# Activation transposes of 40 chunks moved from TensorE to VectorE blocks and a trip through DRAM, with each down product one step later

## The chip, the cores and the metric

The kernel runs on one core of a Trainium2 chip. The metric is device time in microseconds (us) of one execution, the median of several. A profile is one further execution, taken with the hardware profiler. TensorE's matmuls appear as PE, its weight loads as PEld, VectorE as DVE, ScalarE as ACT, GpSimd as POOL and the queue of DMA issues of SyncE as SP.

## The reference

`x` is 64 batches of 32 rows with 512 columns, so 2048 rows of 512 in float32. Four residual stages follow each other; each adds its result to x. What matters here is the first:

```
gate = x @ W_gate.T + 0.5 * (x @ A_gate[b].T) @ B_gate[b].T     # F = 1376 columns
up   = x @ W_up.T   + 0.5 * (x @ A_up[b].T)   @ B_up[b].T
act  = silu(gate) * up
x    = x + act @ W_down.T + 0.5 * (act @ A_down[b].T) @ B_down[b].T
```

`b` picks one of 16 adapters of rank 16 for each batch. Then come a 32x32 mix of the rows of a batch by one of 16 matrices, a 512x512 product with two of eight gated experts of rank 16, and a second 32x32 mix.

## The kernel before

The 2048 rows are 16 tiles (`NT`) of 128 rows, four batches each. The 1376 columns of the hidden layer are three chunks (`CHUNKS`, `NC` = 3): n = 0 has 352 columns (three pieces of 128, 128 and 96), n = 1 and n = 2 have 512 (four pieces of 128). A step `s` is one chunk of one tile, 48 steps in all; the first six (`FREE`) run in an order of their own, then s = 3i + n.

Every product is made of three matmuls on high and low parts of both operands (`product`), because each operand is split into a rounded high part, which ScalarE casts (`hi`), and the remainder, which VectorE subtracts (`lo`). The stationary operand is loaded anew for each of the three.

A step on TensorE is `gate` (12 matmuls), `up` (12), `adapters` (4, after which the chunk's gate and up values are complete, `s_gu`), and then for a finished chunk the product with W_down. ScalarE applies silu to the gate half, VectorE multiplies by the up half. The result `act` has rows on partitions and hidden columns in the free dimension, but the down product contracts over hidden columns. So `transpose_act` turns each piece with a TensorE transpose against the identity into PSUM (`act_t`), ScalarE and VectorE split it into `act_hl` (two buffers), and `down` uses the pieces as stationary operands: two halves of `down_ps`, three matmuls each, 288 columns wide. In step s TensorE transposes chunk s-1 in the middle and multiplies it by W_down at the end. After a tile's third chunk, `mask_td`, `transpose_td` and `down_adapters` add the rank-16 part and VectorE adds the residual (`x1`).

The order is written out by hand. `lane_jobs(s)` is the list of jobs that ScalarE and VectorE both follow, in that order; `gathers(s)` is GpSimd's list of indirect loads (`b` the adapter's B columns, `a` its A matrices, `bd` its B_down, `w13` the mixing matrices), followed on GpSimd by the low part of one tile's mixing matrix (`low_bd`, steps 10 to 25). SyncE's queue issues the plain transfers in program order and stops at each wait: `store_bd` (steps 10 to 25) waits for `low_bd`, `store_tile` for a tile's residual. From step 45 on the loads for the second part of the kernel are issued there.

Of the kernel before, what the change touches and what calls it, by code (L numbers as in the profile page):

```python
# [123 lines left out]

PLAIN = NT - 3
# [17 lines left out]
def down_no(s):  # L143

    i, n = ORDER[s]
    return i * NC + n

# [41 lines left out]
def gathers(s):  # L189

    if s < FREE:
        return {-1: a_items(0, 0) + [("b", 0), ("b", 1)] + a_items(1) + a_items(0, 1),
                0: [("b", 2)],
                1: [("b", 3)],
                2: [("bd", 0), ("b", 4)],
                3: [("b", 5)] + a_items(2),
                4: [("b", 6)],
                5: [("bd", 1)]}[s]
    i, n = ORDER[s]
    out = []  # L200
    if s + 1 < STEPS:
        out.append(("b", s + 1))
    if n < 2 and i + 1 < NT:
        out += a_items(i + 1)[n * TB // 2:(n + 1) * TB // 2]
    if n == 2:
        out.append(("bd", i))
    if 0 <= s - W13_FIRST < NT:
        out.append(("w13", s - W13_FIRST))
    return out


def lane_jobs(s):
# [17 lines left out]
    i, n = divmod(s, NC)  # L230
    jobs = []
    if n == 0:
        if i < NT:
            jobs.append(("tm", i))
        jobs.append(("act", s - 1))
        if i < NT:
            jobs += [("t", i), ("bd", i - 1), ("tdm", i - 1), ("gate", s), ("b", s + 1)]
        else:
            jobs += [("bd", i - 1), ("tdm", i - 1), ("td", i - 1), ("x1", i - 1)]
    elif n == 1:  # L240
        jobs += [("td", i - 1), ("act", s - 1), ("x1", i - 1)]
        if i + 1 < NT:
            jobs.append(("x", i + 1, 0))
        jobs += [("gate", s), ("b", s + 1)]
    else:
        jobs.append(("act", s - 1))
        if i + 1 < NT:
            jobs.append(("at", i + 1))
        jobs.append(("gate", s))
        if i + 1 < NT:  # L250
            jobs += [("b", s + 1), ("adt", i + 1)]
    return jobs
# [5 lines left out]
def bass_conditioned_residual_chain(nc, x_t, x_rows, it_cond, it_lang, wgu, wd, a_all, a_gu, a_d, b_d,  # L258
# [6 lines left out]
    with ExitStack() as ctx:  # L265
# [25 lines left out]
        x_scratch = nc.dram_tensor("x_after_l0", [ROWS, H], F32, kind="Internal").ap()  # L291
        bd_scratch = nc.dram_tensor("bd13", [NT, P, 4 * P], F32, kind="Internal").ap()
# [29 lines left out]
        act_hl = sb("act_hl", [2, 2, HC, P], F32R, mem_a)  # L322
# [99 lines left out]
        s_actt = sem("s_actt")  # L422
        s_hi = sem("s_hi")
# [80 lines left out]
        def act_of(s):  # L504
            w = width(ORDER[s][1])
            return act[:, slot(s), 0:w] if slot(s) < 2 else x_res[:, 1, 0:w]

# [79 lines left out]
        def _(sp):  # L587
# [45 lines left out]

            for s in range(-1, STEPS):
# [29 lines left out]
                if s == 5:  # L664
                    store_tile(0)
                    sp.wait_ge(s_actt, down_no(2) + 1)
                    sp.dma_start(x_res[:, 1, :], x_rows[P:2 * P, :]).then_inc(s_xin[1], 16)
                if s >= FREE:
                    i, n = ORDER[s]
                    if n == 1:  # L670
                        store_tile(i - 1)
                    if n == 2:
# [111 lines left out]
        def _(sc):  # L784
# [15 lines left out]
            def job_hi(job):  # L800
# [3 lines left out]
                if kind == "gate":  # L804
                    s = job[1]
                    sc.wait_ge(s_gu, s + 1)
                    if slot_before(s) is not None:
                        sc.wait_ge(s_actt, down_no(slot_before(s)) + 1)
                    sc.activation(act_of(s), gate_of(s), ACT.Silu).then_inc(s_silu, 1)  # L809
                elif kind == "act":  # L810
                    d = job[1]
                    sc.wait_ge(s_actt, d + 1)
# [119 lines left out]
        def _(ve):  # L932
# [64 lines left out]

            def job_lo(job):
# [14 lines left out]
                if kind == "gate":  # L1013
# [3 lines left out]
                    ve.tensor_tensor(a, a, up_of(s), ALU.mult).then_inc(s_mul, 1)  # L1017
                    return
                ve.wait_ge(s_hi, split_no[job])
                if kind == "act":  # L1020
                    d = job[1]
                    for k, j0, j1 in act_blocks(d):
# [158 lines left out]
        def _(pe):  # L1181
# [66 lines left out]
            def transpose_act(d):  # L1248
# [3 lines left out]
                if d >= 1:  # L1252
                    pe.wait_ge(s_lo, s_lo_of(("act", d - 1)))
# [5 lines left out]
            def down(d):  # L1259
# [9 lines left out]
                for j, f in enumerate(pieces_of(n)):  # L1269
# [3 lines left out]
                    a_hl = [act_hl[0:w, d % 2, part, j, :] for part in range(2)]  # L1273
# [139 lines left out]
            for s in range(FREE + 1, STEPS):  # L1413
                i, n = ORDER[s]
                gate(s, 0, HC // 2)
                if n == 1:
# [4 lines left out]
                if n == 1:  # L1421
# [112 lines left out]
```

## Time and profile before

| what | value |
|---|---|
| median of 3 runs | 579.16 us (578.42 to 579.67) |
| the profiled execution's own time | 578.63 us |
| its span, first to last instruction | 576.5 us |
| mean granted TensorE clock | 1.000 |
| PE busy | 566.9 us (98%) |
| DVE, ACT, POOL busy | 303.0, 205.1, 224.7 us |

The own time is 2.1 us longer than the span, and the median lies 0.5 us above the own time. The engines' busy times overlap. A busy PE is not PE at its best rate: matmuls are pipelined, so how often one starts tells more than how long one lasts.

### The profile page before, as it was taken

What the parts mean: (1) busy time and instruction counts of PE and PEld (TensorE: products, weight loads), DVE (VectorE), ACT (ScalarE), POOL (GpSimd) and SP (SyncE); (2) the same over time, 40 slices, a digit from 0 to 9 for tenths busy, and PEclk for the clock granted to TensorE, in tenths of its full rate; (3) what the DMA queues carried; (4) which work ended last, traced back from release to release, by engine and by line L of the source; (5) the groups of instructions that cost most, each with busy time, mean ns of one, the idle gap of its engine ahead of it and who ended that gap; (6) DMA issues with size and microseconds to landing.
All of it is one profiled execution on the core that took longest, in us unless ns stands there. A gap on an engine that the chain in (4) does not pass through costs nothing.

```text
span 576.5 us, 8783 instructions
## 1 busy us (share of the span) xinstructions
PE 566.9 (98%) x3367; PEld 513.1 (89%) x3367; DVE 303.0 (53%) x695; ACT 205.1 (36%) x413; POOL 224.7 (39%) x229
## 2 busy tenths in 40 slices
PE   6999999999999999999999999999999999999997
PEld 6889989898989898989898989898989899999995
DVE  6797344444444444444444444444444667777876
ACT  5774233333333333332323232323232533333330
POOL 5751053747474747341414141414140212443430
PEclk9999999999999999999999999999999999999999
DMA  8983352444444444452424242424241821234322
GB/s 296 362 265 121 109 163 78 143 135 141 135 143 134 143 135 142 132 157 76 139 78 138 77 139 76 139 77 138 77 139 73 305 81 55 74 133 143 110 92 74
DMA packets 34585, 77.38 MB, mean 134 GB/s; under 512 B 5232, under 2 KB 8944, under 8 KB 34544
## 3 DMA queue, kind: packets, MB, share of 16 engines
q0 software_dynamic: 10880, 37.23, 20.7%
q1 hardware_dynamic: 23520, 39.54, 20.2%
q8 instruction: 27, 0.44, 0.3%
q14 instruction: 14, 0.11, 0.1%
q10 hardware_dynamic: 144, 0.04, 0.0%
HBM read 64.22 MB, written 12.58 MB: 133 GB/s over the span
## 4 chain that ended last, share of the span: by engine, by line
PE 92%; DVE 3%; POOL 2%; DMA 2%; issue 1%; ACT 0%; DVEq 0%; ACTq 0%
PE gu_ps L1186 13%; PE gu_ps L1185 13%; PE gu_ps L1184 13%; PE down_ps L1184 8%; PE down_ps L1185 8%; PE down_ps L1186 8%; PE l_ps L1184 5%; PE l_ps L1185 5%; PE l_ps L1186 5%; PE act_t L1256 3%; PE gu_ps L1192 3%; PE gu_ps L1191 3%; POOL a_raw L696 1%; PE x2t_ps L1310 1%; DMA a_raw<-a_all,idx_batch 1%; DVE w_sb L971 1%
## 5 line engine op out<-in xcount | busy, mean ns | idle before, releaser
L696 POOL DMA_INDIRECT b_sel_raw<-b_gu,idx_rank x48 | 47.3, 985 | 184.5 <-PE gu_ps L1192 174.0
L1184 PE MATMUL down_ps<-wd_sb,act_hl 128*128 128x288 f32 (+1 forms) x352 | 105.0, 298 | 0.2 <-DVE wd_sb L971 0.2
L1184 PE MATMUL gu_ps<-w_sb,xt 128*128 128x512 f32 x256 | 104.2, 407 | 0.0
L1185 PE MATMUL down_ps<-wd_sb,act_hl 128*128 128x288 f32 (+1 forms) x352 | 103.8, 295 | 0.0
L1186 PE MATMUL down_ps<-wd_sb,act_hl 128*128 128x288 f32 (+1 forms) x352 | 103.6, 294 | 0.0
L1186 PE MATMUL gu_ps<-w_sb,xt 128*128 128x512 f32 x256 | 100.8, 394 | 0.0
L1185 PE MATMUL gu_ps<-w_sb,xt 128*128 128x512 f32 x256 | 100.5, 393 | 0.0
L696 POOL DMA_INDIRECT a_raw<-a_all,idx_batch x60 | 71.8, 1197 | 52.1 <-DVE wd_sb L971 38.1
L818 ACT CAST act_hl<-act_t 128x256 fp32r<-128x256 f32 (+1 forms) x64 | 27.3, 453 | 132.2 <-PE act_t L1256 130.9
L809 ACT ACTIVATE act<-gu_ps 128x512 f32<-128x512 f32 (+1 forms) x47 | 26.1, 555 | 124.0 <-PE gu_ps L1192 124.0
L971 DVE TENSOR_TENSOR act_hl<-act_t,act_hl 128x256 fp32r<-128x256 f32 (+1 forms) x64 | 32.0, 521 | 71.2 <-ACT act_hl L818 71.1
L1184 PEld LDWEIGHTS down_ps<-wd_sb,act_hl 128*128 128x128 f32 (+1 forms) x352 | 66.1, 188 | 1.9 <-DVE wd_sb L971 0.6
L1185 PEld LDWEIGHTS down_ps<-wd_sb,act_hl 128*128 128x128 f32 (+1 forms) x352 | 66.1, 188 | 1.2
L1186 PEld LDWEIGHTS down_ps<-wd_sb,act_hl 128*128 128x128 f32 (+1 forms) x352 | 66.0, 188 | 0.0
L1017 DVE TENSOR_TENSOR act<-act,gu_ps 128x512 f32<-128x512 f32 (+1 forms) x47 | 29.8, 634 | 66.5 <-ACT act L809 66.5
L971 DVE TENSOR_TENSOR b_sel<-b_sel_raw,b_sel 128x1024 fp32r<-128x1024 f32 (+1 forms) x48 | 53.6, 1116 | 10.5 <-ACT b_sel L793 10.5
L1186 PEld LDWEIGHTS gu_ps<-w_sb,xt 128*128 128x128 f32 x256 | 48.0, 187 | 10.7
L1184 PEld LDWEIGHTS gu_ps<-w_sb,xt 128*128 128x128 f32 x256 | 48.1, 188 | 8.4
L1185 PEld LDWEIGHTS gu_ps<-w_sb,xt 128*128 128x128 f32 x256 | 48.3, 189 | 7.2
L793 ACT CAST b_sel<-b_sel_raw 128x1024 fp32r<-128x1024 f32 (+1 forms) x48 | 45.7, 952 | 1.5 <-DMA b_sel_raw<-b_gu,idx_rank 1.3
L1184 PE MATMUL l_ps<-w2ra_hl,x2t_hl 128*128 128x328 f32 (+1 forms) x128 | 41.6, 325 | 0.4 <-issue 0.2
L1185 PE MATMUL l_ps<-w2ra_hl,x2t_hl 128*128 128x328 f32 (+1 forms) x128 | 39.7, 310 | 0.0
(150 smaller groups left out, 1093.6 us busy)
## 6 DMA issues: line engine op xcount, KB each, us to landing
xt_raw<-x_t SPq DMA_DIRECT2D x16, 256.0 KB, 2.5
w_sb_raw<-wgu SPq DMA_DIRECT2D x16, 256.0 KB, 7.5
x_res<-x_rows SPq DMA_DIRECT2D x16, 256.0 KB, 2.9
x_after_l<-x_res SPq DMA_DIRECT2D x16, 256.0 KB, 2.3
bd<-bd_hl SPq DMA_DIRECT2D x16, 256.0 KB, 2.0
x<-x_after_l SPq DMA_DIRECT2D x16, 256.0 KB, 2.8
bd_hl<-bd SPq DMA_DIRECT2D x16, 256.0 KB, 3.9
out<-y SPq DMA_DIRECT2D x15, 256.0 KB, 2.0
```

The costliest lines, as they stand in the source:

```text
L696: nc.gpsimd.indirect_dma_start(out=dst, out_offset=None, in_=table, in_offset=bass.IndirectOffsetOnAxis(ap=idx, axis=0)).then_inc(s, 16)
L793: sc.copy(out_, in_).then_inc(s_hi, 1)
L809: sc.activation(act_of(s), gate_of(s), ACT.Silu).then_inc(s_silu, 1)
L818: ins = sc.copy(act_hl[0:k, d % 2, 0, j0:j1, :], act_t[0:k, j0:j1, :])
L971: return ve.tensor_tensor(out_, raw, high.bitcast(F32), ALU.subtract)
L1017: ve.tensor_tensor(a, a, up_of(s), ALU.mult).then_inc(s_mul, 1)
L1184: pe.matmul(out_, stationary[0], moving[0], start=start, stop=False, skip_group_check=True)
L1185: pe.matmul(out_, stationary[0], moving[1], start=False, stop=False, skip_group_check=True)
L1186: return pe.matmul(out_, stationary[1], moving[0], start=False, stop=stop, skip_group_check=True)
L1191: pe.matmul(out_, stationary, moving[0], start=False, stop=False, skip_group_check=True)
L1192: return pe.matmul(out_, stationary, moving[1], start=False, stop=True, skip_group_check=True)
L1256: mm = pe.transpose(act_t[0:w, j, :], act_of(s)[:, j * P:j * P + w], ident)
```

## The change

`MOVED` is range(6, 46): chunks 6 to 45, 40 of the 48. For them TensorE's transpose is gone. Behind the multiplication VectorE transposes `act` in square blocks of 32x32 (`blocks`) into `act_blk`, which is the other slot of `act`; all moved chunks now use slot 1. A block transpose leaves each value in its group of 32 partitions. SyncE's queue therefore writes the result to DRAM (`act_scratch`, 128 rows of 512 numbers, 256 KB) and, when this has landed, reads it back in four transfers, one for each group of 32 partitions (`move_act`), each row in runs of 128 numbers (512 bytes). It arrives in the low half of `act_hl`, ScalarE casts the high part from there, and VectorE subtracts in place. In a row of the result the pieces alternate: number 4n + j belongs to row n of piece j, so `stationary_of` reads a stationary operand with a step of four numbers (16 bytes), where `act_hl` before had its 128 numbers side by side. Chunks with three pieces leave every fourth place unused.

In step s TensorE now multiplies chunk s-2 by W_down instead of s-1. The tile's end (`td`, `down_adapters`, `x1`, `store_tile`) moves from n = 1 to n = 2 of the next tile, the split of `bd` from n = 0 to n = 1, and its gather on GpSimd from the step n = 2 of its own tile to n = 0 of the next, behind that step's `a` gathers.

```diff
+MOVED = range(FREE, STEPS - 2)
@@ gathers
-    if n == 2:
+    if n == 0 and i >= 3:
+        out.append(("bd", i - 1))
+    if s == STEPS - 1:
         out.append(("bd", i))
@@ lane_jobs
+    last = [("act", s - 1)] if s - 1 not in MOVED else []
+    acts = ([("act", s - 2)] if s - 2 in MOVED else []) + last
+        return [("tm", i)] + acts + [("t", i), ("gate", s), ("b", s + 1)]
+        return acts + x + ([("bd", i - 1)] if i > 2 else []) + [("gate", s)] + tdm + [("b", s + 1)]
+    jobs = [("td", i - 1)] + acts[:1] + [("x1", i - 1)] + acts[1:]
@@ stationary and split
+        def stationary_of(d, part, j, w):
+            a = act_hl[0:w, d % 2, part, :, :]
+            if d in MOVED:
+                return a.rearrange("p a n -> p (a n)").rearrange("p (n j) -> p j n", j=HC)[:, j, :]
+            return a[:, j, :]
@@ sync
+            def move_act(d):
+                sp.wait_ge(s_blocks, moved(d))
+                if d - 2 in MOVED:
+                    sp.wait_ge(*act_in(d - 2))
+                sp.dma_start(act_scratch[d % 2, :, :], act_blk).then_inc(s_aout, 16)
+                if d >= 2:
+                    sp.wait_ge(s_d, d - 1)
+                sp.wait_ge(s_aout, 16 * moved(d))
+                for j in range(HC):
+                    rows = slice(j * CH, (j + 1) * CH)
+                    sp.dma_start(act_raw[rows, d % 2, 1, :, :],
+                                 act_scratch[d % 2, :, j * P:(j + 1) * P].rearrange("(b f) n -> f b n", b=TB)
+                                 ).then_inc(s_ain[d % 2], 16)
+                if s - 1 in MOVED:
+                    move_act(s - 1)
@@ scalar
+                    if d in MOVED:
+                        sc.wait_ge(*act_in(d))
+                        cols = split_cols(d)
+                        hi(cols(act_hl[:, d % 2, 0, :, :]), cols(act_raw[:, d % 2, 1, :, :]))
+                        return
@@ vector
+            def blocks(s):
+                ve.wait_ge(s_mul, s + 1)
...
+                    ve.wait_ge(s_aout, 16 * moved(s - 1))
...
+                by_place = act_blk.rearrange("p (j r a) -> p j a r", j=TB, a=HC)
+                ins = ve.transpose(by_place[:, :, 0:full, :],
+                                   act_of(s)[:, 0:whole_cols].rearrange("p (a j f) -> p j a f", j=TB, f=CH))
...
+                    if s in MOVED:
+                        blocks(s)
@@ tensor, the loop over steps
-                if n == 1:
+                if n == 2:
                     transpose_td(i - 1)
-                transpose_act(s - 1)
+                if s == STEPS - 1:
+                    transpose_act(s - 1)
-                down(s - 1)
+                if s - 2 in MOVED:
+                    down(s - 2)
                 if n == 0:
                     adapters(s)
+            down(STEPS - 2)
```

On TensorE, in the middle of a step with n = 0, between the last gate matmuls (`gu_ps_0`) and the first up matmuls (`gu_ps_1`), before:

```order
L1184 MATMUL gu_ps_0<-wg_sb,xt 128x480
L1185 MATMUL gu_ps_0<-wg_sb,xt 128x480
L1186 MATMUL gu_ps_0<-wg_sb,xt 128x480
L1256 MATMUL act_t<-ident_sb,act 128x128 x4
L1184 MATMUL gu_ps_1<-wu_sb,xt 128x352
L1185 MATMUL gu_ps_1<-wu_sb,xt 128x352
```

The same engine near the end of such a step in the changed kernel, from the last up matmuls through the transpose of the adapters' part to the down product:

```order
L1269 MATMUL gu_ps_1<-wu_sb,xt 128x352
L1270 MATMUL gu_ps_1<-wu_sb,xt 128x352
L1271 MATMUL gu_ps_1<-wu_sb,xt 128x352
L1319 MATMUL t_ps<-ident_sb,t_m 128x128 x2
L1269 MATMUL down_ps<-wd_sb,act_hl 128x288
L1270 MATMUL down_ps<-wd_sb,act_hl 128x288
L1271 MATMUL down_ps<-wd_sb,act_hl 128x288
```

The transposes into `act_t` have gone from these steps; the down product stands where it stood, and is that of the chunk one earlier.

On SyncE's queue, one tile in the part where mixing matrices are stored (`bd<-bd_hl`), before:

```order
L615 DMA xt_raw<-x_t 128x512
L625 DMA bd<-bd_hl 128x512 x2
L590 DMA x_after_l<-x_res 128x512
L625 DMA bd<-bd_hl 128x512
L674 DMA x_res<-x_rows 128x512
```

and in the changed kernel, where `act_blocks` is the DRAM buffer:

```order
L650 DMA xt_raw<-x_t 128x512
L660 DMA bd<-bd_hl 128x512
L674 DMA act_blocks<-act 128x512
L680 DMA act_hl_raw<-act_blocks 32x4x128 x4
L660 DMA bd<-bd_hl 128x512
L674 DMA act_blocks<-act 128x512
L680 DMA act_hl_raw<-act_blocks 32x4x128 x4
L660 DMA bd<-bd_hl 128x512
L674 DMA act_blocks<-act 128x512
L680 DMA act_hl_raw<-act_blocks 32x4x128 x4
L625 DMA x_after_l<-x_res 128x512
L725 DMA x_res<-x_rows 128x512
```

Five issues have been added for each chunk, each group of them behind the store of a mixing matrix.

On GpSimd, the step n = 0 of the changed kernel in that part (its first row waits for the adapters' matmuls of the step ahead, its second for VectorE's split of the A matrices):

```order
L747 DMA b_sel_raw<-b_gu,idx_rank 128x1024
L747 DMA a_raw<-a_all,idx_batch 128x304 x2
L747 DMA bd_hl_raw<-b_d,idx_rank 128x512
L747 DMA w_raw<-w,idx_ch 128x64
L802 TENSOR_TENSOR bd_hl<-bd_raw,bd_hl 128x256
```

Before, the gather `bd_hl_raw` stood in the step n = 2, which has no `a_raw` gathers. The last row is `low_bd`, for which the store on SyncE waits.

## Rows read from the trace of the kernel before

**Rows 1.** The page: its head and first section, busy time by engine.

```profile
span 576.5 us, 8783 instructions
PE 566.9 (98%) x3367; PEld 513.1 (89%) x3367; DVE 303.0 (53%) x695; ACT 205.1 (36%) x413; POOL 224.7 (39%) x229
```

**Rows 2.** The longest wait of TensorE's matmuls: total us, times, longest.

```profile
PE gu_ps L1184 <- DVE wg_sb L971: 5.5, 1, 5.5
```

**Rows 3.** Busy time by engine in one tile's window (PE, PEld, DVE, ACT, POOL).

```profile
130.92:159.66 28.74, 28.74 (x169) 25.81 (x168) 12.48 (x22) 9.80 (x20) 16.97 (x20) 1.00 0.44 139
```

**Rows 4.** One of TensorE's groups by shape: busy us, mean ns, idle before.

```profile
L1256 PE MATMUL act_t<-ident_sb,act 128*128 128x128 f32 x158 | 24.9, 272 | 0.0
```

**Rows 5.** Timeline of TensorE around one group of transposes: start, us, instruction.

```profile
210.25 0.38 PE L1185 MATMUL gu_ps<-wg_sb,xt 128*128 128x480 f32 x1
210.47 0.38 PE L1186 MATMUL gu_ps<-wg_sb,xt 128*128 128x480 f32 x1
210.68 0.60 PE L1256 MATMUL act_t<-ident_sb,act 128*128 128x128 f32 x4
211.04 0.41 PE L1184 MATMUL gu_ps<-wu_sb,xt 128*128 128x352 f32 x1
211.28 0.32 PE L1185 MATMUL gu_ps<-wu_sb,xt 128*128 128x352 f32 x1
211.44 0.32 PE L1186 MATMUL gu_ps<-wu_sb,xt 128*128 128x352 f32 x1
```

**Rows 6.** Timeline of TensorE, three regular stretches: 128, 288 and 512 columns wide.

```profile
24.97 0.27 PE L1185 MATMUL down_ps<-wg_sb,xt 128*128 128x128 f32 x1
...
26.09 0.27 PE L1186 MATMUL down_ps<-wg_sb,xt 128*128 128x128 f32 x1
...
213.39 0.30 PE L1185 MATMUL down_ps<-wd_sb,act_hl 128*128 128x288 f32 x1
...
215.89 0.29 PE L1186 MATMUL down_ps<-wd_sb,act_hl 128*128 128x288 f32 x1
...
220.75 0.40 PE L1186 MATMUL gu_ps<-w_sb,xt 128*128 128x512 f32 x1
220.98 0.39 PE L1184 MATMUL gu_ps<-w_sb,xt 128*128 128x512 f32 x1
```

**Rows 7.** Timeline of ScalarE: the silu at the start of a step n = 0.

```profile
118.69 0.60 ACT L809 ACTIVATE act<-gu_ps 128x512 f32<-128x512 f32 x1 [2.57 <-PE gu_ps L1192]
```

**Rows 8.** Timeline of VectorE behind that silu.

```profile
119.32 0.69 DVE L1017 TENSOR_TENSOR act<-act,gu_ps 128x512 f32<-128x512 f32 x1 [2.40 <-ACT act L809]
125.58 0.69 DVE L971 TENSOR_TENSOR act_hl<-act_t,act_hl 128x512 fp32r<-128x512 f32 x1 [0.57 <-ACT act_hl L818]
130.28 0.36 DVE L991 TENSOR_TENSOR td<-down_ps,head_sb 128x64 f32<-128x64 f32 x2 [1.58 <-PE down_ps L1186]
```

**Rows 9.** Timeline of GpSimd in the same step, and one bd gather later.

```profile
118.93 0.98 POOL L696 DMA_INDIRECT b_sel_raw<-b_gu,idx_rank  x1 [2.99 <-PE gu_ps L1192]
122.02 0.95 POOL L696 DMA_INDIRECT a_raw<-a_all,idx_batch  x1 [2.12 <-DVE wd_sb L971]
...
125.48 0.76 POOL L751 TENSOR_TENSOR bd_hl<-bd_raw,bd_hl 128x256 fp32r<-128x256 f32 x1
...
140.53 1.36 POOL L696 DMA_INDIRECT bd_hl_raw<-b_d,idx_rank  x1 [0.30 <-issue]
```

**Rows 10.** Timeline of SyncE's queue: two merged stores, and one load.

```profile
126.26 12.28 SPq L625 DMA_DIRECT2D bd<-bd_hl  x2
...
144.28 0.43 SPq L674 DMA_DIRECT2D x_res<-x_rows  x1
```

**Rows 11.** DMA issues by line: count, size, median us from issue to landing.

```profile
x_res<-x_rows SPq DMA_DIRECT2D x16, 256.0 KB, 2.9
x_after_l<-x_res SPq DMA_DIRECT2D x16, 256.0 KB, 2.3
bd_hl<-bd SPq DMA_DIRECT2D x16, 256.0 KB, 3.9
```

More of the change, by code:

```diff
@@ L146, in down_no, with pe_transposed @@
     return i * NC + n
+def pe_transposed(d):
+    return sum(k not in MOVED for k in range(d + 1))
 def gu_done(i):
@@ L230, in lane_jobs @@
     i, n = divmod(s, NC)
-    jobs = []
+    last = [("act", s - 1)] if s - 1 not in MOVED else []
+    if i == NT:
+        return last + [("bd", i - 1), ("tdm", i - 1), ("td", i - 1), ("x1", i - 1)]
+    acts = ([("act", s - 2)] if s - 2 in MOVED else []) + last
     if n == 0:
[L233 to L252, printed above, removed]
+        return [("tm", i)] + acts + [("t", i), ("gate", s), ("b", s + 1)]
+    if n == 1:
+        x = [("x", i + 1, 0)] if i + 1 < NT else []
+        tdm = [("tdm", i - 1)] if i > 2 else []
+        return acts + x + ([("bd", i - 1)] if i > 2 else []) + [("gate", s)] + tdm + [("b", s + 1)]
+    jobs = [("td", i - 1)] + acts[:1] + [("x1", i - 1)] + acts[1:]
+    if i + 1 < NT:
+        return jobs + [("at", i + 1), ("gate", s), ("b", s + 1), ("adt", i + 1)]
+    return jobs + [("gate", s)]
 NO_SPLIT = ("gate", "tm", "tdm", "x1")
@@ L321, in bass_conditioned_residual_chain @@
             pass
-        act_hl = sb("act_hl", [2, 2, HC, P], F32R, mem_a)
+        act_hl, act_raw = sb_raw("act_hl", [2, 2, HC, P], mem_a)
         b_sel, b_raw = sb_raw("b_sel", [2, 2, 2 * H], mem_a)
@@ L422, in bass_conditioned_residual_chain @@
         s_actt = sem("s_actt")
+        s_blocks = sem("s_blocks")
+        s_aout = sem("s_aout")
+        s_ain = [sem(f"s_ain{i}") for i in range(2)]
         s_hi = sem("s_hi")
@@ L505, in act_of, with moved, act_in, split_cols @@
             w = width(ORDER[s][1])
+            if s in MOVED:
+                return act[:, 1, 0:w]
             return act[:, slot(s), 0:w] if slot(s) < 2 else x_res[:, 1, 0:w]
+        act_blk = act[:, 0, :]
+        def moved(d):
+            return d - MOVED[0] + 1
+        def act_in(d):
+            return s_ain[d % 2], 16 * TB * sum(k % 2 == d % 2 for k in MOVED if k <= d)
+        def stationary_of(d, part, j, w):
[3 more added lines that the diff above has]
+            return a[:, j, :]
+        def split_cols(d):
+            n = len(pieces_of(d % NC))
+            def cols(a):
+                return a.rearrange("p a n -> p (a n)").rearrange("p (n j) -> p n j", j=HC)[:, :, 0:n]
+            return cols
         def base_cols(i):
@@ L806, in job_hi @@
                     sc.wait_ge(s_gu, s + 1)
-                    if slot_before(s) is not None:
+                    if s - 1 in MOVED and s in MOVED or s == STEPS - 2:
+                        sc.wait_ge(s_blocks, moved(s - 1))
+                    elif s == STEPS - 1:
+                        sc.wait_ge(s_aout, 16 * len(MOVED))
+                    elif slot_before(s) is not None:
                         sc.wait_ge(s_actt, down_no(slot_before(s)) + 1)
@@ L811, in job_hi @@
                     d = job[1]
-                    sc.wait_ge(s_actt, d + 1)
+                    if d in MOVED:
[3 more added lines that the diff above has]
+                        return
+                    sc.wait_ge(s_actt, pe_transposed(d))
                     if d == 0:
@@ L996, in mask_td @@
                 ins.then_inc(s_tdm, 1)
+            def blocks(s):
+                ve.wait_ge(s_mul, s + 1)
+                if s == MOVED[0]:
+                    ve.wait_ge(s_actt, s)
+                else:
+                    ve.wait_ge(s_aout, 16 * moved(s - 1))
+                whole_cols = width(ORDER[s][1]) // P * P
+                by_place = act_blk.rearrange("p (j r a) -> p j a r", j=TB, a=HC)
+                full = whole_cols // P
+                ins = ve.transpose(by_place[:, :, 0:full, :],
+                                   act_of(s)[:, 0:whole_cols].rearrange("p (a j f) -> p j a f", j=TB, f=CH))
+                left = width(ORDER[s][1]) - whole_cols
+                if left:
+                    ins = ve.transpose(by_place[:, 0:left // CH, full, :],
+                                       act_of(s)[:, whole_cols:].rearrange("p (j f) -> p j f", f=CH))
+                ins.then_inc(s_blocks, 1)
             def job_lo(job):
@@ L1017, in job_lo @@
                     ve.tensor_tensor(a, a, up_of(s), ALU.mult).then_inc(s_mul, 1)
+                    if s in MOVED:
+                        blocks(s)
                     return
@@ L1021, in job_lo @@
                     d = job[1]
+                    if d in MOVED:
+                        cols = split_cols(d)
+                        lo(cols(act_hl[:, d % 2, 1, :, :]), cols(act_raw[:, d % 2, 1, :, :]),
+                           cols(act_hl[:, d % 2, 0, :, :])).then_inc(s_lo, 1)
+                        return
                     for k, j0, j1 in act_blocks(d):
@@ L1251, in transpose_act @@
                 pe.wait_ge(s_mul, s + 1)
-                if d >= 1:
-                    pe.wait_ge(s_lo, s_lo_of(("act", d - 1)))
+                before = max((k for k in range(d) if k not in MOVED), default=None)
+                if before is not None:
+                    pe.wait_ge(s_lo, s_lo_of(("act", before)))
                 for j, f in enumerate(pieces_of(n)):
@@ L1272, in down @@
                         pe.wait_ge(s_lo, s_lo_of(("wd", f)))
-                    a_hl = [act_hl[0:w, d % 2, part, j, :] for part in range(2)]
+                    a_hl = [stationary_of(d, part, j, w) for part in range(2)]
                     for half in range(2):
```

6 lines of the change are left out of this document (3 added, 3 removed).

## The prediction

> **What bounds the kernel now.** I read the page's first section, then TensorE's waits, then its groups and timeline. TensorE is busy for 566.9 of 576.5 us [rows 1], and its waits come to five entries, of which one, at the start, has 5.5 us and the others 0.2 us each [rows 2]. In one tile's window of 28.74 us it is busy for all of it, while VectorE has 12.48 us of work, ScalarE 9.80 and GpSimd 16.97 [rows 3]. So an instruction taken off TensorE in the middle of the kernel shortens the kernel by the time for which it held up the next matmul, as long as nothing that TensorE needs then comes later. What the other engines get is free while they keep their slack.
>
> That time isn't the 272 ns of one transpose [rows 4], since starts overlap. In the timeline the last of the 480-wide matmuls starts at 210.47 and the second 352-wide one at 211.28, so 0.81 us later, with four transposes between [rows 5]. The same step costs 0.22 us behind a 480-wide matmul (210.25 to 210.47) and 0.16 behind a 352-wide one (211.28 to 211.44), so 0.38 without them. The four cost 0.43 us, 0.108 each. The other group of spacings that I need: a 128-wide matmul with its own weight load starts every 0.112 us (ten steps from 24.97 to 26.09), a 288-wide one of the down product every 0.132 (19 steps from 213.39 to 215.89), and a 512-wide one every 0.23 [rows 6].
>
> **Removed.** Chunks 6 to 45 are 14 with three pieces and 26 with four: 42 + 104 = 146 transposes. At 0.108 us this is 15.8 us. All of it is on the path.
>
> **Unchanged in number.** The down products keep their matmuls. The casts and subtractions have about the size that they had; a three-piece chunk has one of each in place of two.
>
> **Added on VectorE.** One block transpose of 512 numbers per partition for each chunk (two instructions where there are three pieces). No row has one. The nearest are the 128x512 multiplication and subtraction, 0.69 us each [rows 8]; I take 0.7. From below, nothing; from above, twice 0.69, since it writes with a step of four numbers. Three per tile are 2.1 to 4.2 us on top of 12.48 in a window of 28.74, so VectorE stays far from full. The job behind it in the step n = 1 is `td`, 0.36 us [rows 8], which TensorE's `transpose_td` needs 1.4 us (six 512-wide matmuls) after the down product ends. Multiplication and transpose lie beside that product (24 matmuls, 3.2 us): 0.6 for silu, 0.7, 0.7, and VectorE is free 1.2 us before `td` may start. With a transpose of over 1.9 us this cover begins to go, and with over 2.9 TensorE waits.
> The Trainium skill (VectorE: DVE Perf Modes, The three transpose paths) gives 311 ns for a 128x128 block transpose of 2-byte numbers and says that it stays within 32x32 blocks; no run here shows it, and the sum doesn't use it.
>
> **Added transfers.** 256 KB out and 256 KB in per chunk, about 9.6 us apart, so 53 GB/s beside the 139 of the window [rows 3]. A 256 KB store takes 2.3 us to landing, loads 2.9 to 3.9 [rows 11]. Does the chunk arrive before its down product? With d the chunk's adapters' end as zero, the product one step later starts for a chunk n = 2 after 18 down matmuls (2.4), gate and up of n = 0 (12 x 0.22 + 12 x 0.16 = 4.5), two transposes (0.2), 24 down matmuls (3.2), four adapter matmuls (0.6), and gate, up and adapters of n = 1 (28 x 0.23 = 6.4): 17.3 us. In the later part of the kernel the chain is silu, multiplication, transpose (2.0), store (2.3 and 0.4 to issue), four issues of 0.43 [rows 10], landing (2.9), cast (0.6) and subtraction (0.7): 10.6 us. That leaves more than 6 us, so no wait.
>
> In steps 10 to 25 SyncE's queue has the store of a mixing matrix ahead of the chunk, and that waits for GpSimd's `low_bd`. It is issued at 126.26, 7.6 us behind the silu at 118.69 [rows 7, 10]. In the changed kernel the `a` gather, which waits for VectorE and sat 2.12 us [rows 9], comes 0.7 later because of the block transpose, and the `bd` gather now stands in this step, 1.36 and 0.30 us [rows 9]. So the store is issued at 9.9, the chunk's at 10.3, lands at 12.6; four issues bring 14.3; landing 17.2; cast 17.8; subtraction 18.5 less the 0.3 by which neighbours on two engines overlap, 18.2. Needed at 17.3, and 17.4 with rounding: TensorE waits about 0.8 us. This happens for n = 2 alone, in five tiles: a chunk n = 0 has neither that wait nor the bd gather ahead of its store, a chunk n = 1 no a gathers. So I charge 4 us. From below: with 2.3 us for the load 0.3 us a tile, 1.5 in all. From above: 3.9 us for each transfer and 1.4 for the block transpose give 4.1 us a tile, 20 in all; that would need each of them at its worst, and I take 10 as this case's end.
>
> **What the down matmul's weight load costs.** Each of the 146 pieces is loaded six times, 876 loads, now with a step of 16 bytes. No row has such a load. What the rows show is the room: loads side by side keep up with a start every 0.112 us, and a down matmul starts every 0.132 [rows 6]. So a load may grow by 20 ns for nothing. At 876 x 18 ns = 15.8 us the whole gain is eaten, which is a load of 0.150 us. From below, nothing. From above, a doubled load: 0.224 against 0.132, 876 x 0.092 = 81 us. In favour of nothing: the moving operand of the same engine is read at 512 numbers in 0.23 us, 2.2 a nanosecond [rows 6], the weights at no more than 128 in 0.112, 1.1 a nanosecond, so the load uses half of the rate that the reads next to it show. Against: that fast read takes four numbers of each 16 bytes, one new 16 bytes every 1.8 ns, and the strided load would need a new one every 0.9 ns. Between ends so far apart I take nothing, being nearer to the row for the same operation, and hold the doubling as the chief rival.
> The Trainium skill speaks against the change here (Advanced Engine Details and Errata, Memory Cachelines): SBUF lines are 16 bytes, and at least two hits on a line are needed to absorb the access latency. By that rule every number of these loads would be a line of its own, with a penalty whose size the page doesn't give. No run so far shows it for weights.
>
> **Sum.** 15.8 off, 4.0 on, nothing for the loads: -11.8 us. The profiled execution goes from 578.63 to 566.8 and its span from 576.5 to 564.7. The median of the runs is 0.5 above the profiled execution, so 567.3 us. The end of the kernel keeps its order but for one product; the queued loads for the second part go ahead of chunk 45, which has 18 us until its product, and I charge nothing.
>
> **The rivals.** (A) The forecast: weight loads hide, few waits. Own range 563.4 (no waits at all) to 573.4; chance 0.55.
> (B) Slower: the strided weight load takes twice as long and becomes the pace of the down product, at the places of the 876 matmuls. It decides from 0.150 us a load on. -15.8 + 81 + 0 (the waits vanish because the product is later) = +65: 644 us. For it speaks that nothing in the trace covers more than 20 ns; against it the spare rate. Chance 0.27. Between (A) and (B), a load of 0.140 to 0.20 us gives -9 to +44; chance 0.08, of which a quarter ends faster and a quarter within 0.2%.
> (C) The way through DRAM is late in every step, not only in 15: SyncE's queue stops for each landing, and each transfer takes 3.9 us or more. For it speaks the full queue in steps 10 to 25; against it the 6 us of slack after. If the two earlier kinds of chunk in those steps wait as well, 1.5 us each, that adds 15 us: 579 to 582. Chance 0.07, half of it within 0.2% or slower.
> (D) The transposes did not matter: they hide in TensorE's own pipeline. The 0.43 us in the timeline say no; 0.03.
>
> **How the numbers follow.** A change of 0.2% (1.2 us) is about what can be told from none. Faster: 0.55 + 0.02 + 0.03 = 0.60, rounded up by what lies between to 0.61; same: 0.02 + 0.02 = 0.04; slower: the rest, 0.35. The likeliest case gives 567.3. Its own range is 563.4 to 573.4, which holds 0.55 alone, so the range must reach to (B), up to 645; it leaves out little but a load that more than doubles.
>
> **What would show it.** TensorE busy for about 551 us. Starts of down matmuls 0.132 us apart as before under (A), 0.2 or more under (B); the recorded time of a weight load tells nothing by itself, since it contains latency. Waits of TensorE on the low half of `act_hl`, about 0.8 us in tiles 4 to 8 and none later; a block transpose of 0.7 to 1.4 us; the chunk's store issued 2.5 us behind its silu in late steps and 10 us in the five early ones. The prediction is wrong if the spacing of the down product changes, or if TensorE waits in the later tiles.

## The result and the profile after

The changed kernel takes 653.45 us (median of four runs, 652.87 to 654.84), the kernel before 578.92 beside it (four runs). The ratio is 1.129 with an interval of 1.1266 to 1.1313: 74.5 us slower, where 567.3 was forecast and 645 was the upper end of the range. The page's head and first section, against [rows 1]:

```profile
span 651.0 us, 8755 instructions
PE 638.0 (98%) x3221; PEld 586.1 (90%) x3221; DVE 333.4 (51%) x735; ACT 202.7 (31%) x399; POOL 209.1 (32%) x229
```

The 146 matmuls are gone (3367 to 3221), and TensorE is busy for 71.1 us more, at a mean granted clock of 0.997. So nearly all of the time went into work that takes longer, not into waits. The waits of TensorE's matmuls (total us, times, longest), against [rows 2]:

```profile
PE gu_ps L1269 <- DVE wg_sb L1031: 5.4, 1, 5.4
PE l_ps L1269 <- POOL x_hl L807: 2.6, 1, 2.6
```

One wait of size is new: 2.6 us at the start of the second part, on GpSimd's low half of `x_hl`. The other entries have 0.5 us or less each, and none is on `act_hl`. The timeline of TensorE, one down product, against [rows 6]:

```profile
278.27 0.30 PE L1269 MATMUL down_ps<-wd_sb,act_hl 128*128 128x288 f32 x1
278.40 0.40 PE L1270 MATMUL down_ps<-wd_sb,act_hl 128*128 128x288 f32 x1
...
283.54 0.40 PE L1271 MATMUL down_ps<-wd_sb,act_hl 128*128 128x288 f32 x1
283.77 0.40 PE L1269 MATMUL gu_ps<-w_sb,xt 128*128 128x512 f32 x1
```

From 278.40 to 283.54 there are 22 steps, so a start every 0.2336 us where there was one every 0.132. A 288-wide matmul now keeps the pace of a 512-wide one (0.23). Only the first step, from 278.27 to 278.40, still has 0.13. The operation that changed shows in the view of the tile `act_hl` (duration min/median/max in ns, first and last start, forms): its weight loads.

```profile
L1269 PEld LDWEIGHTS down_ps<-wd_sb,act_hl x352: 186/329/334, 37.2 to 548.5; 128*128 128x128 f32 x160, 96*128 96x128 f32 x16
```

The shortest, 186 ns, belongs to the chunks whose operand still lies side by side; the median of 329 is the strided form. The sum closes: 876 loads x 0.1015 us is 88.9, less 15.8 for the transposes, plus the new wait of 2.6, gives 75.7, and 74.5 was measured. If in each of the 40 products one step keeps its 0.13 us, 836 loads pay: 84.9, and 71.7 in all, to which the clock (0.997 over 651.0 us) adds 2.0 at most.

### The profile page after: what moved, and what is told of

Same layout as the page of the kernel before. It is cut to its first block, busy times and chain, and to the rows that moved or that the text cites. A ratio compares the mean times of both kernels' runs of the same rounds, so it can differ in the third digit from the quotient of the medians.

```text
span 651.0 us, 8755 instructions
## 1 busy us (share of the span) xinstructions
PE 638.0 (98%) x3221; PEld 586.1 (90%) x3221; DVE 333.4 (51%) x735; ACT 202.7 (31%) x399; POOL 209.1 (32%) x229
## 4 chain that ended last, share of the span: by engine, by line
PE 90%; DMA 3%; POOL 2%; DVE 2%; SPq 1%; issue 1%; ACT 0%; DVEq 0%; ACTq 0%
PE down_ps L1270 11%; PE down_ps L1271 11%; PE down_ps L1269 11%; PE gu_ps L1269 11%; PE gu_ps L1271 11%; PE gu_ps L1270 11%; PE l_ps L1269 4%; PE l_ps L1270 4%; PE l_ps L1271 4%; PE gu_ps L1277 3%; PE gu_ps L1276 3%; DMA act_blocks<-act 1%; POOL a_raw L747 1%; PE x2t_ps L1396 1%; DMA b_sel_raw<-b_gu,idx_rank 1%
## 5 line engine op out<-in xcount | busy, mean ns | idle before, releaser
L1270 PE MATMUL down_ps<-wd_sb,act_hl 128*128 128x288 f32 (+1 forms) x352 | 133.5, 379 | 0.0
L1271 PE MATMUL down_ps<-wd_sb,act_hl 128*128 128x288 f32 (+1 forms) x352 | 133.4, 379 | 0.0
L1269 PE MATMUL down_ps<-wd_sb,act_hl 128*128 128x288 f32 (+1 forms) x352 | 132.8, 377 | 0.3 <-DVE wd_sb L1031 0.3
L1269 PEld LDWEIGHTS down_ps<-wd_sb,act_hl 128*128 128x128 f32 (+1 forms) x352 | 106.7, 303 | 2.3 <-DVE wd_sb L1031 0.7
L1271 PEld LDWEIGHTS down_ps<-wd_sb,act_hl 128*128 128x128 f32 (+1 forms) x352 | 107.6, 306 | 0.0
L1270 PEld LDWEIGHTS down_ps<-wd_sb,act_hl 128*128 128x128 f32 (+1 forms) x352 | 107.1, 304 | 0.2
L747 POOL DMA_INDIRECT a_raw<-a_all,idx_batch x60 | 61.2, 1021 | 64.6 <-DVE wd_sb L1031 50.6
L1269 PE MATMUL l_ps<-w2ra_hl,x2t_hl 128*128 128x328 f32 (+1 forms) x128 | 41.6, 325 | 0.4 <-issue 0.2
L1068 DVE STREAM_TRANSPOSE act<-act 128x512 f32<-128x512 f32 (+1 forms) x40 | 38.1, 952 | 7.0 <-DMA act_blocks<-act 5.8
L1270 PE MATMUL l_ps<-w2ra_hl,x2t_hl 128*128 128x328 f32 (+1 forms) x128 | 39.7, 310 | 0.0
L1271 PE MATMUL l_ps<-w2ra_hl,x2t_hl 128*128 128x328 f32 (+1 forms) x128 | 39.6, 310 | 0.0
```

Of the source, the lines that this page charges most:

```text
L747: nc.gpsimd.indirect_dma_start(out=dst, out_offset=None, in_=table, in_offset=bass.IndirectOffsetOnAxis(ap=idx, axis=0)).then_inc(s, 16)
L1068: ins = ve.transpose(by_place[:, :, 0:full, :], act_of(s)[:, 0:whole_cols].rearrange("p (a j f) -> p j a f", j=TB, f=CH))
L1269: pe.matmul(out_, stationary[0], moving[0], start=start, stop=False, skip_group_check=True)
L1270: pe.matmul(out_, stationary[0], moving[1], start=False, stop=False, skip_group_check=True)
L1271: return pe.matmul(out_, stationary[1], moving[0], start=False, stop=stop, skip_group_check=True)
```

## The experiments

Each group of runs has its own runs of the kernel before: 579.41 for the first four kernels, 578.81 for the next four, 578.99 for the last two. Two theories stood against each other. L: every one of the 876 loads costs 0.1 us because of its step of 16 bytes, and the rest of the change costs little. T: the rest of the change (256 KB out to DRAM and back in each step, over the same buffers and queues) slows the down product or makes it wait.

**The changed kernel with operands side by side.** `stationary_of` and the split of `act_hl` no longer use the step:

```diff
             a = act_hl[0:w, d % 2, part, :, :]
-            if d in MOVED:
-                return a.rearrange("p a n -> p (a n)").rearrange("p (n j) -> p j n", j=HC)[:, j, :]
             return a[:, j, :]
...
-            n = len(pieces_of(d % NC))
+            n = HC
```

> The changed kernel in which the down product of the moved chunks reads each stationary operand as 128 numbers side by side (step of 4 bytes instead of 16), and the split always covers all four places; the operands are then in the wrong order, so the output is not the reference's. Theory 1 (the 16-byte step of the weight load makes it the pace of the down product): its matmuls start every 0.132 us again instead of 0.233, and the time is that of before less 15.8 us for the transposes plus a few us of waits, 563 to 570 us. Theory 2 (something else in the changed kernel slows the down product: operands that arrive by DMA, reads of act_hl by three engines at once, the later place in the order): the spacing stays at 0.233 and the time near 653 us.

Measured: 583.89 us (580.92 to 586.66), ratio 1.0078 (1.004 to 1.0116). Down matmuls start 0.13 us apart again (two rows of TensorE's timeline), so L holds for the 71 us of busy time:

```profile
172.62 0.29 PE L1267 MATMUL down_ps<-wd_sb,act_hl 128*128 128x288 f32 x1
172.75 0.29 PE L1268 MATMUL down_ps<-wd_sb,act_hl 128*128 128x288 f32 x1
```

But 583.89 is above the 563 to 570 of the expectation, and 20 us above what the removal alone should leave. The waits of TensorE and of SyncE's queue in this kernel (the profiled execution is the longest of the four, 586.66 us):

```profile
PE down_ps L1267 <- DVE act_hl L1029: 10.5, 6, 2.6
...
PE gu_ps L1274 <- DVE b_sel L1029: 2.5, 1, 2.5
...
SPq L675 <- DMA act_blocks<-act: 120.6, 40, 6.1
```

The 10.5 us on `act_hl` are the wait that the forecast had priced at 4.0. Five of the six are on a chunk n = 2, as forecast, with 2.56, 1.27, 2.35, 2.33 and 1.84 us. The timeline of ScalarE, SyncE's queue and TensorE in one of these steps:

```profile
115.95 0.60 ACT L862 ACTIVATE act<-gu_ps 128x512 f32<-128x512 f32 x1 [2.77 <-PE gu_ps L1275]
126.17 0.33 SPq L658 DMA_DIRECT2D bd<-bd_hl  x1
126.59 0.38 SPq L672 DMA_DIRECT2D act_blocks<-act  x1
128.98 1.74 SPq L678 DMA_DIRECT2D act_hl_raw<-act_blocks  x4
...
132.91 0.39 PE L1275 MATMUL gu_ps<-b_sel,t_hl 128*128 128x512 f32 x1
...
134.46 0.62 ACT L842 CAST act_hl<-act_hl_raw 128x512 fp32r<-128x512 f32 x1 [5.78 <-DMA act_hl_raw<-act_blocks]
...
135.85 0.40 PE L1267 MATMUL down_ps<-wd_sb,act_hl 128*128 128x288 f32 x1 [2.56 <-DVE act_hl L1029]
```

With the silu as zero, the mixing matrix's store is issued at 10.2, the chunk's at 10.6, the loads at 13.0 to 14.8, the cast starts at 18.5 and the product at 19.9. It could have started at 17.2.

The wait on `b_sel` is of another kind. There is one buffer for the blocks. VectorE stood still until the chunk stored before had landed, and so the split of `b_sel` came late (VectorE's timeline):

```profile
163.31 0.63 DVE L1066 STREAM_TRANSPOSE act<-act 128x256 f32<-128x256 f32 x1 [5.01 <-DMA act_blocks<-act]
...
163.97 1.20 DVE L1029 TENSOR_TENSOR b_sel<-b_sel_raw,b_sel 128x1024 fp32r<-128x1024 f32 x1
```

TensorE waits 2.50 us for it, until 165.22, works on four matmuls, and waits 1.27 for `act_hl`, until 168.28. Busy time in windows of 2 us there (PE, PEld, DVE, ACT, POOL, then the granted clock, the DMA engines' share and GB/s):

```profile
162.00:164.00 2.00, 0.72 (x4) 0.26 (x2) 0.69 (x3) 0.00 (x0) 1.80 (x4) 1.00 0.73 287
164.00:166.00 2.00, 0.78 (x3) 0.64 (x4) 1.17 (x2) 0.00 (x0) 0.00 (x0) 0.89 0.42 116
166.00:168.00 2.00, 1.01 (x3) 0.29 (x1) 0.47 (x1) 1.11 (x3) 0.71 (x1) 0.50 0.74 278
168.00:170.00 2.00, 1.72 (x7) 1.72 (x8) 2.00 (x4) 2.00 (x5) 1.34 (x2) 0.50 0.50 127
170.00:172.00 2.00, 2.00 (x10) 2.00 (x9) 1.16 (x2) 0.28 (x1) 1.49 (x3) 0.50 0.67 208
172.00:174.00 2.00, 2.00 (x14) 1.91 (x13) 0.40 (x3) 0.00 (x0) 0.00 (x0) 0.90 0.67 255
```

Right behind the first wait the granted clock falls, and it is 0.50 (1.2 GHz, the lower level) from 166 to 172 although TensorE works again from 168.3 on; the down product runs at 0.24 us a matmul in place of 0.132. So a wait here costs more than its own length. Over the whole span the mean clock is 0.988, which is at most 7.0 us of 584.8: 1.2% of it, if TensorE could have used every cycle.

**The kernel before with the strided operand alone**, steps of 16 and of 8 bytes, in the same 876 loads:

```diff
                     a_hl = [act_hl[0:w, d % 2, part, j, :] for part in range(2)]
+                    if 6 <= d < STEPS - 2:
+                        a_hl = [act_hl[0:w, d % 2, part, :, :].rearrange("p a n -> p (a n)").rearrange(
+                            "p (n j) -> p j n", j=HC)[:, j, :] for part in range(2)]
```

For 8 bytes the last two lines are `...[:, j:j + 2 * (P - 1) + 1:2]`.

> The kernel before with one thing changed: for chunks 6 to 45 the stationary operands of the down product are read with a step of four numbers (16 bytes), so that the output is not the reference's. Theory 1: 876 matmuls start every 0.233 us instead of 0.132, so 579 + 876 x 0.1015 = 668 us (665 to 671). Theory 2: no change, 579 us.

> The kernel before with a step of two numbers (8 bytes) in the same 876 weight loads; the output is not the reference's. If what counts is that each number lies in a 16-byte line of its own (two numbers of a line in a row are enough): no change, 578 to 580 us. If any step other than one costs the same: 668 us, as with a step of four. If the cost grows with the distance read over: between, 590 to 640 us.

Measured: 665.42 us (664.95 to 665.86) with 16 bytes, ratio 1.1486 (1.147 to 1.1503), and 579.17 (578.92 to 579.75) with 8, ratio 0.9999 (0.9985 to 1.0013). TensorE's timeline with 16 bytes:

```profile
213.09 0.40 PE L1184 MATMUL down_ps<-wd_sb,act_hl 128*128 128x288 f32 x1
213.33 0.40 PE L1185 MATMUL down_ps<-wd_sb,act_hl 128*128 128x288 f32 x1
```

No transfer to DRAM and back, no block transpose and no new order is in this kernel, and the spacing is that of the changed one. The loss is 86.0 us, 98 ns for each load. With that T falls as the cause of the 74.5 us. With 8 bytes the matmuls start every 0.133 us (19 steps of TensorE's timeline):

```profile
214.28 0.30 PE L1185 MATMUL down_ps<-wd_sb,act_hl 128*128 128x288 f32 x1
...
216.81 0.30 PE L1186 MATMUL down_ps<-wd_sb,act_hl 128*128 128x288 f32 x1
```

**Pieces side by side, stored in runs of 128 bytes.** Four stores in place of one put the pieces in order on the way out, four loads with rows of 2 KB bring them in:

```diff
-                sp.dma_start(act_scratch[d % 2, :, :], act_blk).then_inc(s_aout, 16)
+                for b in range(TB):
+                    sp.dma_start(act_scratch[d % 2, :, :].rearrange("(f j) (a b r) -> b f (j a) r", j=TB, a=HC, b=TB)[b],
+                                 act[b * CH:(b + 1) * CH, 0, :].rearrange("p (x r) -> p x r", r=CH)).then_inc(s_aout, 16)
```

> The changed kernel with the pieces put side by side on the way: the block transpose writes runs of 32 numbers, four stores (one for each group of 32 partitions) write runs of 128 bytes to DRAM, four loads read 2 KB a row, and the stationary operand has a step of one number. Computes the reference. Theory 1: down matmuls start every 0.132 us, 563 to 572 us if the more numerous short packets (2048 of 128 bytes a chunk) arrive within the 6 us of slack, block transposes of 0.7 instead of 1.1 us. Theory 2: near 650 us. If the short packets are too slow for the slack, TensorE waits for the low half of act_hl in every step and the time lies between.

Measured: 598.37 us (595.86 to 602.89), ratio 1.0338 (1.0289 to 1.0386). The weight loads are cheap (ten down matmuls in 1.33 us, from 275.63 to 276.96), but the stores are late, which is the third case of the expectation. VectorE's waits on a transfer, against 9.1 us in five waits in the kernel with operands side by side and one store:

```profile
DVE act L1067 <- DMA act_blocks<-act: 32.2, 13, 5.2
```

TensorE waits 8.8 us for `act_hl`, 6.9 for `b_sel` and 3.0 for `td`, and its mean clock is 0.974 in the profiled execution.

**The chunk's transfers ahead of the mixing matrix.** The first experiment again, with `move_act(s - 1)` written before the store of `bd` in SyncE's loop:

```diff
+                if s - 1 in MOVED:
+                    move_act(s - 1)
                 if 0 <= s - W13_FIRST - 2 < NT:
...
-                if s - 1 in MOVED:
-                    move_act(s - 1)
```

> As e1_after_step1 (the changed kernel with stationary operands of the moved chunks read side by side; output not the reference's), and on SyncE's queue a chunk's store and loads are issued ahead of the mixing matrix's store of the same step, not behind it. In e1 the chunk's store came some 8 to 10 us behind its silu in steps 10 to 25, and TensorE waited for the low half of act_hl and for what VectorE did late. If that place in the queue is where the missing 20 us went: 563 to 569 us, no waits on act_hl. If the transfers themselves are too slow, or VectorE is too full: 578 to 584 us, as e1.

Measured: 570.25 us (567.94 to 570.34), ratio 0.9854 (0.9838 to 0.9871), so 13.6 less than the first experiment by the medians (13.0 when each is taken against its own runs of the kernel before), and 1.3 above the expected 563 to 569. SyncE's queue at the same place, behind a silu at 114.79:

```profile
117.29 0.33 SPq L672 DMA_DIRECT2D act_blocks<-act  x1
121.74 1.75 SPq L678 DMA_DIRECT2D act_hl_raw<-act_blocks  x4
```

The store goes out 2.5 us behind the silu and the loads 6.9 (before 10.6 and 13.0), and the down product starts at 131.97, 17.2 us behind the silu, without a wait. TensorE's waits now have no entry for `act_hl`. The two largest that the kernel before hasn't sit at the end of the first part:

```profile
PE l_ps L1267 <- POOL x_hl L805: 2.6, 1, 2.6
PE down_ps L1274 <- DVE td_hl L1029: 1.2, 1, 1.2
```

In the 50 us from 430 to 480 TensorE is busy for 46.02, at a clock of 0.97. This profile is of the shortest execution, 567.94 us; the other three took 570.24 to 570.34.

**Steps of 12 and of 32 bytes in the kernel before**, the edit of above with a step of 3 and of 8 numbers (that of 8 reads `w1_sb` and covers chunks 6 to 43).

> The kernel before with a step of three numbers (12 bytes) in the 876 weight loads; output not the reference's. A step of four cost 86 us, a step of two nothing. If a load takes as long as it meets new 16-byte lines (three lines for four numbers, so 0.233 x 3/4 = 0.175 us a load against 0.132): 876 x 0.043 = 38 us more, 613 to 621 us. If each pair in one line is enough to hide it all: 579. If all steps above two cost the same: 665.

> The kernel before with a step of eight numbers (32 bytes) in the weight loads of chunks 6 to 43 (834 loads), read from a weight tile that holds enough numbers (w1_sb); output not the reference's. If only a line of its own for each number counts, as much as a step of four: 834 x 0.1015 = 85 us, 660 to 665 us. If the distance counts, a doubled load again, 0.466 us: 850 us.

Measured: 616.31 us (615.67 to 616.44) and 667.59 (666.88 to 667.97), ratios 1.0647 (1.0629 to 1.0664) and 1.1532 (1.1512 to 1.1551). TensorE's timelines, 12 bytes and then 32:

```profile
217.78 0.34 PE L1186 MATMUL down_ps<-wd_sb,act_hl 128*128 128x288 f32 x1
217.96 0.34 PE L1184 MATMUL down_ps<-wd_sb,act_hl 128*128 128x288 f32 x1
218.13 0.34 PE L1185 MATMUL down_ps<-wd_sb,act_hl 128*128 128x288 f32 x1
```

```profile
212.73 0.41 PE L1184 MATMUL down_ps<-wd_sb,w_sb 128*128 128x288 f32 x1
212.97 0.41 PE L1185 MATMUL down_ps<-wd_sb,w_sb 128*128 128x288 f32 x1
```

A start every 0.175 us with 12 bytes and every 0.246 with 32. Counted in pieces of 16 bytes that 128 numbers touch, the steps of 1, 2, 3, 4 and 8 numbers meet 32, 64, 96, 128 and 128. With 0.233 / 128 = 1.82 ns for each, 96 give 0.175, as measured and as expected before the run. By the same estimate 64 give 0.117, under the 0.132 between plain down matmuls, so nothing should show, and nothing did. Whether a load with a step of 8 bytes really takes 0.117 no run shows, since it is hidden. Twice the step does not double the load once more. That 32 bytes cost 5% more than 16 (667.59 us, above the expected 660 to 665) is not explained; this kernel also reads its operands from another tile.

**Pairs of pieces interleaved, in runs of 256 bytes, with the new order of transfers.** Since a step of 8 bytes is free, two pieces may share it: VectorE writes the block transpose with `by_place = act_blk.rearrange("p (j h r l) -> p h j l r", j=TB, h=2, l=2)`, and the down product reads

```diff
             a = act_hl[0:w, d % 2, part, :, :]
             if d in MOVED:
-                return a.rearrange("p a n -> p (a n)").rearrange("p (n j) -> p j n", j=HC)[:, j, :]
+                return a.rearrange("p (h l) n -> p h (l n)", l=2)[:, j // 2, :].rearrange("p (n l) -> p l n", l=2)[:, j % 2, :]
             return a[:, j, :]
```

> Computes the reference. The changed kernel with pairs of pieces interleaved (a step of two numbers in the weight load), four stores a chunk in runs of 256 bytes, four loads of 2 KB rows, and the chunk's transfers ahead of the mixing matrix's store. If a step of two is free and the queue was the other cost: 563 to 572 us, faster than both. If 1024 packets of 256 bytes a chunk are still too slow: TensorE waits for act_hl, 575 to 590 us.

Measured: 572.10 us (571.78 to 573.46), ratio 0.9892 (0.9876 to 0.9909), at the upper end of the expected range. Here the end of the first part can be read (timelines of ScalarE, TensorE and GpSimd, then the window of 50 us):

```profile
445.28 0.73 ACT L958 CAST w2ra_hl<-w2ra_hl_raw 128x648 fp32r<-128x648 f32 x1 [0.46 <-DMA w2ra_hl_raw<-w2ra_t]
445.92 0.26 ACT L845 CAST td_hl<-t_ps 128x128 fp32r<-128x128 f32 x1
...
447.26 0.39 PE L1276 MATMUL down_ps<-bd_hl,td_hl 128*128 128x256 f32 x1 [1.96 <-DVE td_hl L1032]
...
448.28 0.94 POOL L748 DMA_INDIRECT bd_hl_raw<-b_d,idx_rank  x1 [16.07 <-PE down_ps L1277]
449.25 2.49 POOL L808 TENSOR_TENSOR x_hl<-x,x_hl 128x512 fp32r<-128x512 f32 x2
```

```profile
430.00:480.00 50.00, 45.28 (x268) 40.59 (x266) 28.30 (x63) 17.47 (x32) 8.76 (x8) 0.93 0.44 143
```

ScalarE's cast of `td_hl` for tile 14 stands behind the casts of the second part's weights, which wait for their transfers. GpSimd's low half of `x_hl`, for which TensorE waits 2.6 us, stands behind the gather of tile 15's `bd`, which waited 16.07 us for the adapters' part of tile 14's down product. Both orders come from the step by which the down product was moved: the tile's end went one step later, and these jobs kept their places.

**The same two kernels with the end in another order.** ScalarE's and VectorE's splits of `w2ra` go from the end of step 46 to the last job of step 47, behind those of tile 14, and the last `bd` gather goes behind `x_hl` (ScalarE's and GpSimd's part of the edit; VectorE's is alike):

```diff
-    if s == STEPS - 1:
-        out.append(("bd", i))
...
                     low_x1(1)
+                    gather_item(("bd", NT - 1))
...
+                        for n in range(HC):
+                            high_w2(n)
                     if job == ("td", NT - 1):
```

> Computes the reference. As e8_store256_act_first, and at the end of the first part ScalarE and VectorE split the second part's weights (w2ra) behind the jobs of tile 14 instead of ahead of them, and GpSimd gathers bd of tile 15 behind the low parts of x1 instead of ahead. In e8 TensorE waited 2.0 us for td_hl and 2.6 us for the low part of x1 there, and its clock fell behind these waits (0.93 in the window 430 to 480). If those two places are what is left: 564 to 568 us. If they only uncover other waits at the same place: 570 to 572.

> The same edit of the end on e5_step1_act_first (stationary operands side by side, output not the reference's). If nothing but the transposes' 15.8 us is left of the change: a span of 560.7 us, so 563 to 565 us. If the end keeps a wait: 568 to 570.

Measured: 564.81 us (564.70 to 565.24) for the kernel with pairs of pieces, ratio 0.9754 (0.9741 to 0.9767), and 563.49 (563.02 to 565.58) for the one with operands side by side, which doesn't undo the alternation of the pieces, ratio 0.9727 (0.9712 to 0.9742). Both lie in the expected ranges. The span of the second is 561.1 to 561.7 us in three of four executions, where 560.7 was expected; the fourth, the profiled one, has 563.7 and still waits 1.0 us for `x_hl`. The first is the version to take, 14.2 us below the kernel before and 88.6 below the changed one. Its page, its largest new wait and the window of the end:

```profile
span 563.0 us, 8901 instructions
PE 551.5 (98%) x3221; PEld 499.2 (89%) x3221; DVE 324.5 (58%) x761; ACT 204.7 (36%) x399; POOL 216.8 (39%) x229
```

```profile
PE down_ps L1267 <- DVE act_hl L1031: 0.8, 1, 0.8
```

```profile
430.00:480.00 50.00, 49.71 (x314) 45.70 (x313) 31.02 (x87) 20.18 (x39) 12.22 (x10) 1.00 0.46 154
```

TensorE is busy for 15.4 us less than in [rows 1]. Beside the waits of the kernel before it has this one of 0.8 and two of 0.6 and 0.5, on `wg_sb` and `x_res`, all three in the first 96 us. In the 50 us from 430 to 480 it is busy for 49.71 in place of 45.28, at a clock of 1.00 in place of 0.93.

## Why the prediction was wrong

**The step that failed is the price of the strided weight load.** The prediction said "Between ends so far apart I take nothing, being nearer to the row for the same operation". That term of the sum stood at nothing. It was 86.0 us when measured alone: the load costs 0.233 us where 0.150 already eats the gain, and rival (B), which had a chance of 0.27, is what happened. Its working stands: its 644 us had a load of 0.224, and the measured 0.233 adds 8 us, the wait at the end 2.6. That is also why the result lies above the range, whose upper end was this rival with a load of 0.224. The argument that misled was the moving operand's rate of 2.2 numbers a nanosecond. It counted numbers, and the runs with 8, 12 and 16 bytes show that what counts is how many new 16 bytes a load touches. The prediction's own sentence against itself had that right: the moving operand took a new 16 bytes every 1.8 ns, the strided load wanted one every 0.9, and it got one every 1.82. So 128 x 1.8 = 0.23 us could have been worked out from the rows of the kernel before. That the moving operand is itself held to that rate by its reads is not shown; the two figures may agree by chance. The Trainium skill (Advanced Engine Details and Errata, Memory Cachelines) has the same in kind: SBUF lines of 16 bytes, and at least two hits on a line to absorb the access latency. The runs agree: two hits on each line (8 bytes) cost 0 us, one (16 bytes) 86.

**The transposes.** 15.8 us was right: 14.2 and 15.5 us were gained once the rest was nearly out of the way.

**The waits of the early steps: right place, price too small, and invisible in the result.** In the changed kernel, slower down products (18 and 24 matmuls between, 0.1 us each) gave the chunk 4.1 us more, and there was no wait on `act_hl`. The timeline of SyncE's queue there, behind a silu at 120.86:

```profile
130.66 0.33 SPq L660 DMA_DIRECT2D bd<-bd_hl  x1
131.08 0.38 SPq L674 DMA_DIRECT2D act_blocks<-act  x1
133.46 1.74 SPq L680 DMA_DIRECT2D act_hl_raw<-act_blocks  x4
```

That is 9.8, 10.2 and 12.6 us behind the silu, where the prediction had 9.9, 10.3 and 12.6. The down product starts at 142.15, 21.3 behind it. With the load made plain the product is due at 17.2 (forecast 17.3) and comes at 19.9, so 2.6 us late and not 0.8: the queue's items are 0.4 later, the last load lands 3.7 us behind its issue and not 2.9, and from the cast's start to the product it takes 1.4 us and not 1.0, since here the subtraction starts 0.65 us behind the cast (134.46 and 135.11). The term was five times 0.8. With the load made plain there are six waits on `act_hl` with 10.5 us, one on `b_sel` with 2.5, and what the clock takes behind them; the kernel that only changes the queue's order is 13.6 us faster by the medians, and no wait on `act_hl` is left. The prediction said of its upper end of 20 us that it "would need each of them at its worst".

**The end was charged nothing, and it costs too.** The prediction looked at the queued loads for the second part and chunk 45, not at ScalarE's and GpSimd's order around tile 14's jobs. In the two faster kernels the reordered end gives 7.3 us (572.10 to 564.81) and 6.8 (570.25 to 563.49). The waits themselves were 2.0 + 2.6 and 1.2 + 2.6; the clock stood at 0.93 and 0.97 in that window, and at 1.00 with the new order, and it is the likely rest. In the changed kernel as it was, the end costs less: its waits there are 0.2 and 2.6 us, and a clock of 0.83 from 525 to 535 is worth 1.7 us at most.

**Block transpose and landings.** These groups of the changed kernel (busy us, mean ns, idle before) and its transfers (KB, median us to landing) answer to the prices in the text:

```profile
L1068 DVE STREAM_TRANSPOSE act<-act 128x512 f32<-128x512 f32 x26 | 29.0, 1117 | 6.5 <-DMA act_blocks<-act 5.8
```

```profile
act_blocks<-act SPq DMA_DIRECT2D x40, 256.0 KB, 3.0
act_hl_raw<-act_blocks SPq DMA_DIRECT2D x160, 64.0 KB, 2.0
```

The block transpose takes 1.12 us in place of 0.7, inside the bounds. By itself it shows no effect: the kernel with 563.49 us keeps it. The store takes 3.0 us in place of 2.3. In the kernel with operands side by side SyncE's queue waits up to 6.1 us for a store, and such a store is what VectorE stood still for, having one buffer.

**What stays open.** Between the stores in runs of 128 bytes (598.37) and of 256 (572.10) the order of the queue changed as well, so how much of the 26 us belongs to the size of the runs isn't told apart. The nearest pairs: with the old order, four stores in runs of 128 bytes are 14.5 us slower than one store (598.37 and 583.89); with the new order, four in runs of 256 bytes are 1.9 slower than one (572.10 and 570.25), and 1.3 with the reordered end. Why single stores took up to 6 us to land isn't shown. A second buffer for the blocks, which would take VectorE's wait away, wasn't tried.

## What to carry to other kernels

Price a weight load with a step by the 16-byte pieces that its 128 columns touch, 1.8 ns each (measured with 96 and 128 pieces), against the spacing of the matmuls that it has to hide behind: for 4-byte numbers and 288 columns a step of two is free, a step of four costs 0.1 us each time. Where a layout forces a step, move part of it elsewhere until two numbers of each piece are used. When a product is moved by a step, write out for each queue what now stands ahead of what it needs, at the ends of loops too, and count a wait of TensorE at more than its length, since the granted clock may be at 1.2 GHz for some microseconds after it, as it was here.

## What was unexpected in the hardware

- Weight loads of 128 columns of 4-byte numbers, ahead of 288-wide matmuls: a start every 0.132 us (the load is hidden) for steps of 4 and 8 bytes, 0.175 for 12, 0.233 for 16, 0.246 for 32.
- A 128x512 block transpose on VectorE takes 1.12 us when written with a step of 16 bytes; with a step of 8 bytes, as two of 128x256, it takes 0.43 each, so 0.86. With a step of 16 bytes 128x256 takes 0.65.
- After a wait of 2.50 us the granted clock fell, and with a second one of 1.27 soon after it stood at 0.50 for six microseconds, during the last four of which TensorE was working.
